# Three of sixteen normalisation tiles on GpSimd, and layer 3's low-rank parts merged inside a normalisation

## The reference, cut to what matters

```python
def _layernorm(x, axis=-1, eps=1e-05):
    m = jnp.mean(x, axis=axis, keepdims=True)
    v = jnp.var(x, axis=axis, keepdims=True)
    return (x - m) / jnp.sqrt(v + eps)

x = _layernorm(x + stage(x, ...), axis=-1)        # twelve times
```

```python
def _lora(t, down, up, alpha):
    return t @ down @ up * (LORA_W * alpha[0] / RANK)
q_in = x @ Wq + _lora(x, q_down, q_up, q_alpha)
k_in = org_ctx @ Wk + _lora(org_ctx, k_down, k_up, k_alpha)
v_in = org_ctx @ Wv + _lora(org_ctx, v_down, v_up, v_alpha)
...
return out @ Wo + bo + _lora(out, o_down, o_up, o_alpha)
```

## Time and profile before

| | us |
|---|---|
| median of 3 runs | 2552.9 |
| lowest, highest | 2545.34, 2553.57 |
| profiled execution | 2537.7 |
| span in the profile | 2535.8 |

### The profile page before, as it was taken

How to read it: one execution, slowest core, us unless ns; L and a number is a source line. 1 busy time by engine, 2 the same in 40 slices (tenths; PEclk the granted TensorE clock), 3 DMA queues, 4 the chain that set the end, 5 groups by cost and what they waited for, 6 DMA issues and landing times. The chain is left out here.

```text
span 2535.8 us, 36942 instructions
## 1 busy us (share of the span) xinstructions
PE 2066.5 (81%) x12688; PEld 1249.8 (49%) x12688; DVE 1552.3 (61%) x3620; ACT 1175.2 (46%) x2304; POOL 762.3 (30%) x938
## 2 busy tenths in 40 slices
PE   5874996768748888997889889775899898677898
PEld 4663662225612324664444444463334466566755
DVE  5867348989848884555554545354567444745676
ACT  3443437644436664224767666533345422133445
POOL 0420005543331100002655555442644100044213
PEclk8985997988959998998999999876789899698899
DMA  1000000000042200002323322102121000200000
GB/s 46 31 7 1 1 1 6 1 28 27 1 117 47 47 2 1 1 1 89 84 72 80 84 71 72 56 1 46 43 55 31 1 1 18 81 1 1 1 1 18
DMA packets 39034, 80.36 MB, mean 32 GB/s; under 512 B 7392, under 2 KB 21728, under 8 KB 37952
## 3 DMA queue, kind: packets, MB, share of 16 engines
q1 hardware_dynamic: 36384, 75.00, 11.1%
q10 hardware_dynamic: 2464, 2.99, 0.5%
HBM read 51.75 MB, written 7.34 MB: 23 GB/s over the span
## 5 line engine op out<-in xcount | busy, mean ns | idle before, releaser
L740 ACT ACTIVATE spt<-P 128x1024 f32<-128x1024 f32 (+3 forms) x256 | 220.9, 863 | 186.0 <-PE P L594 186.0
L707 DVE TENSOR_REDUCE smf<-P 128x2 f32<-128x1024 f32 (+3 forms) x256 | 254.5, 1020 | 47.4 <-PE P L583 24.1
L2274 PEld LDWEIGHTS P<-W,e_h 128*128 128x128 f32 (+1 forms) x1952 | 214.7, 191 | 45.7 <-issue 36.4
L1094 POOL TENSOR_TENSOR d_e<-d_e,d_rc 128x512 f32<-128x512 f32 (+3 forms) x256 | 179.6, 723 | 174.1 <-DVE d_rc L1000 142.8
L2258 PE MATMUL P<-XT,W 128*128 128x512 f32 x424 | 220.1, 617 | 1.2 <-PEq L230 1.2
L2274 PE MATMUL P<-W,e_h 128*128 128x128 f32 (+1 forms) x1952 | 219.2, 278 | 0.0
L2443 DVE SCALAR_TENSOR_TENSOR X<-P,WE,X 128x128 f32<-128x128 f32 x448 | 126.1, 345 | 131.6 <-PE P L2274 130.4
L1043 ACT ACTIVATE d_e<-d_e,d_mn 128x512 f32<-128x512 f32 (+3 forms) x256 | 141.7, 554 | 130.8 <-DVE d_mn L992 130.4
L2322 ACT ACTIVATE e_g<-P 128x512 f32<-128x512 f32 x148 | 88.4, 597 | 240.8 <-PE P L2258 235.3
L2341 DVE TENSOR_TENSOR e_h<-e_g,P 128x512 f32<-128x512 f32 x148 | 101.1, 685 | 108.8 <-PE P L2262 108.5
L2262 PE MATMUL P<-XT,W 128*128 128x512 f32 x296 | 155.8, 608 | 1.6 <-DVE e_h L2341 1.5
(11 more groups left out here) (390 smaller groups left out, 4154.4 us busy)
## 6 DMA issues: line engine op xcount, KB each, us to landing
d_bt<-in_alibi SPq DMA_DIRECT2D x32, 512.0 KB, 3.8
d_moved<-d_raw SPq DMA_DIRECT2D x256, 64.0 KB, 2.4
ska<-parts_k SPq DMA_DIRECT2D x72, 64.0 KB
sqa<-parts_q SPq DMA_DIRECT2D x72, 64.0 KB
W<-in_w_L_xattn SPq DMA_DIRECT2D x1, 4291.0 KB, 12.9
W<-in_w_L_ffn SPq DMA_DIRECT2D x1, 3333.0 KB, 11.1
W<-in_w_L_ffn SPq DMA_DIRECT2D x1, 3155.0 KB, 10.5
parts_k<-sparts SPq DMA_DIRECT2D x8, 384.0 KB, 2.3
```

What stands on the lines that cost most here:

```text
L707: v.tensor_reduce(MF[:, n % 2, u, :], P[:, bank:bank + 2, 0:wide(u)], AX.X, ALU.max, negate=True).then_inc(s("max"), 1)
L740: a.activation(PT[:, n % 3, :, t, N - late(t):N], P[:, BANK_T:BANK_T + 2, 0:late(t)], ACT.Exp, scale=SC).then_inc(s("exp"), 1)
L1094: last = g.tensor_tensor(e, e, RC[:, n % 2, u, h:h + 1].to_broadcast([128, 128 * (u + 1)]), ALU.mult)
L2274: last = pe.matmul(P[:, PY + j % 4, 128 * t:128 * (t + 1)], HT[rows, q % RING, blk, 128 * t:128 * (t + 1)], w2, start=n == 0, stop=n == le ...
```

## The change

In every normalisation the tiles are dealt out by three tables, one tuple per chunk. VectorE takes 0, 1, 4, 5, 8, 9, 10, 12, 13, ScalarE 2, 3, 6, 7, and GpSimd 11, 14, 15, as soon as the root (with again: both sums) is there. TensorE and SyncE wait for a third semaphore from chunk 2 on. The orders of VectorE and ScalarE stay; ScalarE's apply 2 and 3 are empty.

The phase merge_low_rank is gone. The normalisation after L3_attn gets merge=i + 1. TensorE forms products 0 to 3 (q, k) in banks 4 to 7 before the transposes, and 4 to 7 (v, output) after them, each when its bank's earlier product has been added. VectorE forms al first, adds products 0 and 1 between apply 2 and apply 3 and the other six behind apply 3; its two copies go to ScalarE, which copies all four chunks with activation Copy.

```diff
-    on_v, on_a = (0, 1), (2, 3)
+    on_v, on_a, on_g = ((0, 1), (4, 5), (8, 9, 10), (12, 13)), ((2, 3), (6, 7), (), ()), ((), (), (11,), (14, 15))
+    before = lambda on, c: sum(len(ts) for ts in on[:c + 1])
+    def normalised(eng, c):
+        eng.wait_ge(s("norm_v"), before(on_v, c))
+        eng.wait_ge(s("norm_a"), before(on_a, c))
+        if before(on_g, c):
+            eng.wait_ge(s("norm_g"), before(on_g, c))
...
+        def low_rank(pe, n):
+            if n in (2, 3, 4, 5):
+                r = slice(RANK * (n // 2), RANK * (n // 2 + 1))
+                last = pe.matmul(P[0:CD, 4 + n % 4, :], ww["downs"][r, 0:CD], ww["ups"][r, 512 * (n % 2):512 * (n % 2 + 1)], start=True, stop=True)
+            else:
+                for c in range(4 * (n % 2), 4 * (n % 2) + 4):
+                    m = (ww["ups"][0:RANK, 128 * c:128 * (c + 1)], ww["downs"][0:RANK, :]) if n < 2 else \
+                        (ww["odt"][:, 128 * c:128 * (c + 1)], ww["ou"])
+                    last = pe.matmul(P[:, 4 + n % 4, 128 * (c % 4):128 * (c % 4 + 1)], *m, start=True, stop=True)
+            last.then_inc(s("product"), 1)
...
+            def add_low_rank(ns):
+                for n in ns:
+                    if n == 0:
+                        v.wait_ge(s("al"), 1)
+                    name, rows = (("wqt", 128), ("wk", CD), ("wv", CD), ("wo", 128))[n // 2]
+                    v.wait_ge(s("product"), n + 1)
+                    d = ww[name][0:rows, 512 * (n % 2):512 * (n % 2 + 1)]
+                    v.scalar_tensor_tensor(d, P[0:rows, 4 + n % 4, :], al[0:rows, n // 2:n // 2 + 1], d, ALU.mult, ALU.add).then_inc(s("merged"), 1)
+            if merge is not None:
+                merged_ready(v)
+                v.tensor_scalar(al[:], ww["alpha"], 1.0 / RANK, None, ALU.mult).then_inc(s("al"), 1)
...
             apply(2)
-            if not store:
+            if merge is not None:
+                add_low_rank(range(0, 2))
+            elif not store:
                 copy(1)
             apply(3)
-            if not store:
+            if merge is not None:
+                add_low_rank(range(2, 8))
+            elif not store:
                 copy(3)
...
+            def all_turned():
+                for c in QT_:
+                    o, i_ = turned(a, c)
+                    a.activation(o, i_, ACT.Copy).then_inc(s("xt_a"), 1)
...
+        @block.gpsimd
+        def _(g):
+            if rms or not again:
+                g.wait_ge(s("root"), 1)
+            else:
+                g.wait_ge(s("nmr"), 2)
+            for c in (2, 3):
+                for t in on_g[c]:
+                    scaled(g, t).then_inc(s("norm_g"), 1)
...
         def _(pe):
             if store:
                 return
+            if merge is not None:
+                merged_ready(pe)
+                for n in range(4):
+                    low_rank(pe, n)
             for c in QT_:
-                pe.wait_ge(s("norm_v"), 2 * (c + 1))
-                pe.wait_ge(s("norm_a"), 2 * (c + 1))
+                normalised(pe, c)
                 for t in QT_:
                     last = pe.transpose(P[:, c, 128 * t:128 * (t + 1)], dst[:, 4 * c + t, :], k.ident[:])
                 last.then_inc(s("turned"), 1)
+            if merge is not None:
+                for n in range(4, 8):
+                    pe.wait_ge(s("merged"), n - 3)
+                    low_rank(pe, n)
...
-def merge_low_rank(k, i):
...
     elif name == "L3_xattn":
-        merge_low_rank(k, i)
         context_attention(k, i, Context(heads=NH, dh=64, segs=((0, CTX - IPA), (CTX - IPA, CTX))))
```

More of the change, by code:

```diff
@@ L261, in row_means, with normalise @@
         v.bn_aggr(k.MV[:, t, :], ST[:, n, :]).then_inc(s("row_means"), 1)
-def normalise(k, i, src, dst, eps, rms=False, scale=None, shift=None, store=False, again=None, logits=None):
+def normalise(k, i, src, dst, eps, rms=False, scale=None, shift=None, store=False, again=None, logits=None, merge=None):
     nc = k.nc
@@ L279, in normalise @@
         turned_by_a = (0, 2)
+        if merge is not None:
+            al = sb("al", 4)
+            ww, merged_ready = weights(k, merge)
         @block.sync
@@ L304, in apply @@
             def apply(c):
-                for t in on_v:
-                    t += 4 * c
-                    if again or rms:
-                        v.tensor_scalar(dst[:, t, :], src[:, t, :], mul[:, t:t + 1], add[:, t:t + 1] if again else None, ALU.mult,
-                                        ALU.add if again else ALU.bypass).then_inc(s("norm_v"), 1)
-                    else:
-                        v.tensor_scalar(dst[:, t, :], src[:, t, :], k.MV[:, t, 0:1], mul[:, t:t + 1],
-                                        ALU.subtract, ALU.mult).then_inc(s("norm_v"), 1)
+                for t in on_v[c]:
+                    scaled(v, t).then_inc(s("norm_v"), 1)
             def copy(c):
@@ L354, in apply @@
             def apply(c):
-                for t in on_a:
-                    t += 4 * c
+                for t in on_a[c]:
                     a.activation(dst[:, t, :], src[:, t, :], ACT.Identity, scale=mul[:, t:t + 1],
@@ L377, in _ @@
             apply(1)
-            if not store:
+            if not store and merge is None:
                 copy(0)
@@ L381, in _ @@
             apply(3)
-            if not store:
+            if merge is not None:
+                all_turned()
+            elif not store:
                 copy(2)
+        @block.gpsimd
[7 more added lines that the diff above has]
+                    scaled(g, t).then_inc(s("norm_g"), 1)
         @block.tensor
@@ L2560, in build @@
             if not STAGES[i].endswith("xattn") or STAGES[i] == "L3_xattn":
-                normalise(k, i, k.X, k.X, 1e-5, store=i == LAST - 1, logits=(i + 1, 16) if STAGES[i] == "L3_xattn" else None)
+                normalise(k, i, k.X, k.X, 1e-5, store=i == LAST - 1, logits=(i + 1, 16) if STAGES[i] == "L3_xattn" else None,
+                          merge=i + 1 if STAGES[i] == "L3_attn" else None)
 def run_stage(k, i, name):
```

39 lines of the change are left out of this document (6 added, 33 removed).

## The result

| | before | changed |
|---|---|---|
| median | 2551.5 us (8 runs, 2542.1 to 2555.4) | 2534.6 us (8 runs, 2524.4 to 2540.6) |
| ratio, 95% interval | | 0.9931 [0.9911, 0.9951] |
| profiled execution, span | 2535.8 | 2527.5 |
| granted clock of it, of the median run | 0.895, 0.887 | 0.899, 0.895 |

The change makes the kernel 0.69% faster, 17 us. The prediction was 5 us slower. The last row of the table is the key to what follows: the profiled execution of before was one of the quickest of its kernel, with more of the full clock than most. (The eight runs of before in this table have no clock on record. Its 0.887 is the median of the 69 later runs of before, which stood beside the experiments.) Profile against profile the change is 8.3 us, median against median 17.

A forecast was written before the change was run, and what follows sets the result against it. It took ScalarE's second half to set a normalisation's end. Thirteen phases +7.2, last normalisation +0.9 and merge −3.0 gave +5.1 us on the profiled 2537.7, scaled to 2558 us; range 2546 to 2564.

The forecast's parts named there:

- What bounds a phase: Ordinary normalisation: ScalarE's second half sets the end; without new waits 0.17 or 0.23 us gained, 2.3 over 13 phases.
- What GpSimd's tiles cost: Transposing normalisations: each GpSimd tile during VectorE's stream costs VectorE 0.60 us, making a phase about 0.9 longer.
- The sign named for a failure of this term: Normalising tiles: if VectorE's all stay at 0.342 us, the forecast is wrong in its main term.
- the signs for it: Early phases: VectorE tiles about 0.86 us apart, longest near 1.1; GpSimd's up to 1.0; chunk 1 1.7 after chunk 0.
- The rule cited: SBUF port pair shared by VectorE and GpSimd: an exclusive lock, held by the first issuer for the whole instruction.
- When GpSimd is ready: Thirteen phases: at once in seven, about 0.5 us late in two, 1.5 late in four; sum +7.2 us.
- Last normalisation: Final normalisation, gating the last store: 0.9 us longer, bounds −0.7 and +1.3.
- The merge: Merge inside the normalisation: gain 2.0 us at the slow clock, 4.6 if it rises; taken as −3.0, bounds −1.0 and −6.8.
- From the profile to the median: Whole kernel: profiled execution lies 0.6% under the median; the same share carried over gives 2558 us.
- No interference: Normalisations: GpSimd's tiles do not hold VectorE at this size; −6.0 us, 2547; chance 0.07.
- A stream that holds the lock: Normalisations: GpSimd gets in only after VectorE's seven tiles, each phase +0.07 us; 2552; chance 0.13.
- The clock in the merged phase: Merged normalisation: the clock rises there and stays; +8.1 − 6.8 = +1.3 us, 2554; chance 0.10.
- A dearer hand-over: Normalisations: a GpSimd tile costs VectorE 0.75 us instead of 0.60; +4.5 more, 2563; chance 0.20.

The follow-up runs named there:

- the probe: Changed kernel plus fourteen short phases running VectorE and GpSimd streams alone and side by side; time not compared, VectorE lost 0.04 us per GpSimd scaling at 128 columns.
- the second probe: Changed kernel plus short phases with VectorE's 128-wide scalings beside GpSimd scalings of 192 to 2048 columns; time not compared, VectorE lost 0.11 to 6.58 us each.
- merge only: Changed kernel with tiles dealt eight to VectorE and eight to ScalarE as before, low-rank merge inside the normalisation; 0.9993 of before.
- no GpSimd: Changed kernel with GpSimd's tiles 11, 14 and 15 given to ScalarE, nine staying with VectorE; 0.9959 of before.
- late copy and extra matmuls: Changed kernel, VectorE scaling tiles 12 and 13 before copying chunk 1, four extra matmuls ahead of the transposes; 0.9819 of before, 0.9861 when run again.
- late copy alone: Changed kernel with VectorE scaling tiles 12 and 13 before it copies chunk 1; 0.9910 of before.
- extra matmuls alone: Changed kernel with four extra matmuls ahead of the transposes in 13 normalisations, the merged one excepted; 0.9898 of before.
- split only: Changed kernel with merge_low_rank back as its own phase, tiles still dealt nine, four and three; 0.9930 of before.
- without the merge: Changed kernel with VectorE's tiles 12 and 13 before copy 1, four extra matmuls in all 14 transposing normalisations, merge_low_rank its own phase; 0.9884, again 0.9844 of before.
- the extra matmuls that bring no gain without it: Kernel before with only four extra matmuls added ahead of the transposes, tiles as they were; 1.0017 of before.

## Why the prediction was wrong, point by point

**What bounds a phase.** Right. Without a new wait a phase was to gain 0.17 to 0.23; nine of the thirteen gain 0.18 to 0.30 (7.59 to 7.37, 7.60 to 7.38), and chunk 3 waits for tiles 12 and 13, as the walk had it.

**What GpSimd's tiles cost.** This step failed. It took VectorE's loss at 0.60 a tile, and the probe measures 0.04; in the kernel seven tiles lose 0 to 0.15 over GpSimd's three (1.88 to 2.03, where 1.88 is undisturbed). With that the sum's term of +7.2 for thirteen phases became −7.0, of which some −4 is clock and the rest close to the bound of −2.3. The two rows it rested on are right in themselves: the 2.64 us behind a 2048-wide product and the alternation with 512-wide products come again in the probe, as 3.3 and 0.73 us. The error was to carry them to a 128-wide scaling with two scalars, for which before had no row of the two engines together. The bound of no interference was in the text (−2.3), with a chance of 0.07; that its case came true is not to the forecast's credit. The sign named for a failure of this term came: VectorE's median tile stayed at 340 ns, its longest at 431. Of the signs for it only GpSimd's longest tile came, 1.02 us. The rule cited, that the port is held for the whole instruction, is shown by no run at 128 columns: in the second probe VectorE's tiles go on within GpSimd's instructions up to 1024 columns.

**When GpSimd is ready.** Right and without effect: it is there at once in seven of the thirteen phases (as at 373.5), 0.6 us late in two (as at 55.4) and 1.0 to 1.8 late in four.

**Last normalisation.** Forecast +0.9, bounds −0.7 and +1.3; measured −0.5. It fell with the step above.

**The merge.** Mechanism right. At the slow clock forecast 2.0, measured 1.6; with the clock rising behind the middle of the transposes 4.6, measured 4.9. The first transpose was to start at +6.2 and starts at +5.3 in the changed kernel, whose phase began at a higher clock, and at +6.35 in merge only. Whether the clock rises there is luck of the execution: it did in changed and no GpSimd, in part in the kernel with late copy and extra matmuls (14.4 us, 0.63), not in merge only, late copy alone and extra matmuls alone, and of the two probes, both the changed kernel, in one.

**What was missing.** The clock was weighed in one phase alone, in the merged one. The sum had no term for what a broken or unbroken row of transposes does to it elsewhere. Phase by phase the changed kernel gains 7.0 us in the thirteen, 0.5 in the last, 4.9 in the merged one and 2.6 in the context attention behind it, of which the clock gives 2.6 in the third and some 1.4 in the second, sixth and ninth. That is 15, but the two profiled spans are only 8.3 apart. Stages whose code is the same in both were some 6 to 7 us slower in the changed kernel's profiled execution, most of all the one ahead of the eleventh normalisation, 267.9 us at a clock of 0.80 for 260.7 at 0.83; the same stage ran at 0.87 in the second probe's execution. Between medians it is 17 us: 47 fewer slow microseconds at 0.33 are 15.5 of the 17.6 in the spans, and at equal slow time 1.9 ± 1.0 remain. The line is not an account to the microsecond: no GpSimd stands 7.2 ± 0.7 below that of before, with phases no shorter than the changed kernel's, which stands 1.9 below. Presumably slow microseconds beside other engines' work cost nothing and those on TensorE's path half of themselves; no run parts the two. That the split changes the clock is shown by split only, late copy and the extra matmuls together; that it is the unbroken row and nothing else of the split is argued from what stands in the traces, and from the extra matmuls that bring no gain without it. The fourteenth phase, where the changed kernel's row is less broken too and yet stays long, does not bear it out.

**From the profile to the median.** The share of 0.6% by which the profiled execution lay under the median was carried over as a mere scale. It was 0.008 of granted clock, 41 slow microseconds and at 0.33 some 13 of the 15 us between the spans: the very thing that the change moves.

**The rivals.** No interference (2547) came nearest: its mechanism is the one seen, and its time is 12 us too high for want of the clock. A stream that holds the lock didn't occur: at 56.02 GpSimd starts within VectorE's stream, and both run. The clock in the merged phase rose, as its rival said, but on top of no interference, and in the changed kernel's code not in every execution. A dearer hand-over is refuted. Two sums of the prediction are 0.1 off their own terms (4.6 and half of 4.2 are 6.7, not 6.8; thirteen times 0.07 is 0.9, not 0.8), which moves nothing.

**Beyond both kernels.** Split, late copy and extra matmuls are faster than before and changed: 2504 and 2518 us in two sets of runs, 0.982 and 0.986 of before, and without the merge 2521 and 2512. The merge can stay or go.

## What to carry to other kernels

A price for two engines that share something has to be read, or measured, at the width and kind of operation that the change uses: here it goes from 0.04 to 6.6 us with GpSimd's columns alone. A short wait of TensorE's inside a phase can cost more than its own length, where, as it seems here, the clock behind it hangs on it; so read the granted clock in stages that the change doesn't touch, before and after. And compare many runs by span and granted clock before a profiled execution is taken for the kernel.

## What the runs showed of the hardware

VectorE's and GpSimd's scalings of 128 float32 columns run side by side in SBUF at full pace for VectorE (3.27 against 3.16 us for twelve) and 7% more for GpSimd (2.50 against 2.34 for three). Beside VectorE's 128-wide product of two tensors it is GpSimd that is held up: three scalings take 3.27 instead of 2.34. Wider GpSimd scalings hold VectorE for a growing share of their length: 10% at 192 columns, 6% at 256, 19% at 384, 23% at 512, 36% at 1024, 90% at 2048. A stream of 512-wide scalings on VectorE loses more (0.66 at least) than the 128-wide stream (0.49) beside the same GpSimd instruction. The same code in the same stretch had a granted clock of 0.96 in one execution and 0.88 in another, 6.4 us apart.
